# Short matmul operands filled with zero rows to 128 rows in a four-layer graph network

## The reference

```python
# layer 0: graph convolution, then a top-2 mixture of 64 experts, batch norm
m  = segment_sum((feats * rsqrt(deg_out))[src], dst) * rsqrt(deg_in)
x0 = m @ W_gc + b_gc + feats @ W_res + b_res
h1 = gelu(h @ w1[e] + b1[e]); h2 = h1 @ w2[e] + b2[e]   # for each expert e
# layer 1: mean over neighbours
x1 = feat @ w_self.T + b_self + (segment_sum(feat[src], dst) / deg) @ w_neigh.T
# layer 2: graph convolution with self loops, then a linear layer
x2 = (segment_sum((h * norm)[src], dst) + b_conv) @ W_lin + b_lin
# layer 3: tensor product on the edges, weighted by a small network of each edge's 8 scalars
w  = silu(edge_scalars @ fc_w1 / sqrt(8)) @ fc_w2 / sqrt(64)
```

## Time and profile before

| what | value |
|---|---|
| median of 3 runs | 6222.15 us (6221.89 to 6232.34) |
| span of the profiled execution | 6222.9 us |
| PE busy | 5287.1 us, 85% of the span |
| DVE busy | 3828.5 us, 62% |
| POOL busy | 3825.9 us, 61% |
| ACT busy | 1918.2 us, 31% |
| mean granted clock of TensorE | 0.850 |

### The profile page before, as it was taken

One profiled execution on the slowest core, in us unless ns is written; L12 is line 12 of the kernel. 1 busy time (PEld: TensorE's weight loads), 2 busy tenths in 40 slices (PEclk: granted clock), 3 DMA queues, 4 the chain that ended last, 5 costly groups with the idle time before them and its releaser, 6 DMA issues. The chain is left out here.

```text
span 6222.9 us, 94542 instructions
## 1 busy us (share of the span) xinstructions
PE 5287.1 (85%) x22327; PEld 3472.6 (56%) x22327; DVE 3828.5 (62%) x11568; ACT 1918.2 (31%) x5997; POOL 3825.9 (61%) x3961
## 2 busy tenths in 40 slices
PE   3689999895699994699999978998887799999998
PEld 2554444444488883444444444444333677777777
DVE  8745666556611114555555554555554799999997
ACT  0132222222022220422221242221000766666664
POOL 0157777770266651377777746777776377777771
PEclk9988888875799996888888877777565899999998
DMA  3145555552399982255555544554334366666664
GB/s 150 37 132 146 147 146 149 146 137 59 121 319 318 318 291 86 84 148 146 148 148 144 150 94 137 148 146 135 105 106 90 103 187 188 187 188 187 190 187 92
DMA packets 632253, 955.04 MB, mean 153 GB/s; under 512 B 203781, under 2 KB 472147, under 8 KB 631066
## 3 DMA queue, kind: packets, MB, share of 16 engines
q0 software_dynamic: 180864, 480.03, 28.2%
q1 hardware_dynamic: 444479, 458.06, 23.9%
q10 hardware_dynamic: 6460, 12.03, 0.6%
HBM read 772.58 MB, written 182.80 MB: 154 GB/s over the span
## 5 line engine op out<-in xcount | busy, mean ns | idle before, releaser
L688 POOL DMA_INDIRECT agg_msg<-table,agg_idx x2496 | 2362.0, 946 | 839.7 <-issue 677.5
L798 PE MATMUL bank<-agg_msg,agg_hot 128*125 128x256 f32 (+1 forms) x4992 | 1944.9, 506 | 299.5 <-DMA agg_msg<-table,agg_idx 179.4
L798 PEld LDWEIGHTS bank<-agg_msg,agg_hot 128*125 128x125 f32 x4992 | 979.5, 230 | 1246.8 <-DVE agg_hot L705 695.4
L717 DVE TENSOR_TENSOR acc<-acc,bank 125x256 f32 x2496 | 1050.3, 421 | 1005.3 <-PE bank L798 970.4
L1643 POOL DMA_INDIRECT tp_src<-table,tp_idx x832 | 920.5, 1106 | 294.8 <-issue 254.1
L1657 ACT ACTIVATE tp_hots<-tp_hot,tp_weight 128x125 f32<-128x125 f32 x2496 | 814.0, 390 | 391.3 <-PE bank L1672 362.5
L705 DVE TENSOR_SCALAR agg_hot<-iota_i,dst_w 128x126 f32<-128x126 f32 x2496 | 763.7, 306 | 0.0
L1672 PEld LDWEIGHTS bank<-tp_msg,tp_hots 128*125 128x125 f32 x4992 | 680.3, 189 | 47.7
L1672 PE MATMUL bank<-tp_msg,tp_hots 128*125 128x128 f32 x4992 | 685.0, 274 | 0.0
L826 ACT ACTIVATE agg_made<-bank,agg_made 128x128 f32<-128x128 f32 x786 | 289.0, 368 | 1256.8 <-PE bank L781 1255.2
L1668 PE MATMUL bank<-tp_msg,tp_hot 128*125 128x256 f32 x1664 | 558.5, 418 | 133.5 <-DVE tp_msg L1701 132.3
(11 more groups left out here) (286 smaller groups left out, 5519.4 us busy)
## 6 DMA issues: line engine op xcount, KB each, us to landing
tp_weight<-edge_rows SPq DMA_DIRECT2D x832, 130.0 KB, 2.3
edge_rows<-agg_made SPq DMA_DIRECT2D x262, 390.0 KB, 3.4
acc<-in_L_w_laid_dram SPq DMA_DIRECT2D x162, 512.0 KB
acc<-in_L_gnn_w_dram SPq DMA_DIRECT2D x162, 512.0 KB
agg_msg<-table,agg_idx POOLq DMA_INDIRECT x2496, 2.8
table<-tab_out SPq DMA_DIRECT2D x40, 625.0 KB
tp_src<-table,tp_idx POOLq DMA_INDIRECT x832
expert_rows<-prep_zero SPq DMA_DIRECT2D x5, 2500.0 KB
```

The costliest lines, as they stand in the source:

```text
L688: pool.indirect_dma_start(out=msg[PER * g + r][:, 0:D], out_offset=None, in_=table[:, :], in_offset=bass.IndirectOffsetOnAxis(ap=idx[g][:, ...
L717: dve.tensor_tensor(row, row, bank[0:P, 0:D], ALU.add).then_inc(s_add, 1)
L798: pe.matmul(net.bank[w % BANKS][0:P, 0:sums], hot[w % HOTS][:, 0:P], msg[w][:, :], start=True, stop=True).then_inc(s_sum, 1)
```

## The change

Operands with fewer than 128 rows get 128, with zeros in the rows that held nothing. `fc1` becomes 128 x 128, `fc2`, `scal` and `hid` get 128 partitions, so do `root_b`, `shift_b`, `b2` and the experts' `ones`. The products read all rows; L774's weights get 128 columns and its output and SiLU 128 partitions. Transfers write only the rows that they wrote before. POOL fills the aggregates' tiles with zeros at the start of each aggregate, ahead of its first gather, and SP waits for that before its first load; DVE fills the six `b2` buffers at the start of the experts, and POOL waits for these before each of the first six loads of `b2`.

```diff
-            root_w, root_b = ph.sb("root_w", [Q, 2, D]), ph.sb("root_b", [len(biases), D])
+            root_w, root_b = ph.sb("root_w", [Q, 2, D]), ph.sb("root_b", [Q, D])
...
-        fc1, fc2 = ph.sb("fc1", [8, MUL]), ph.sb("fc2", [MUL, 4, MUL])
-        scal = [ph.sb(f"scal{b}", [8, BATCH * Q]) for b in (0, 1)]
-        hid = [ph.sb(f"hid{b}", [MUL, BATCH * Q]) for b in (0, 1)]
+        fc1, fc2 = ph.sb("fc1", [Q, Q]), ph.sb("fc2", [Q, 4, MUL])
+        scal = [ph.sb(f"scal{b}", [Q, BATCH * Q]) for b in (0, 1)]
+        hid = [ph.sb(f"hid{b}", [Q, BATCH * Q]) for b in (0, 1)]
+        s_empty = ph.sem("empty")
...
             def _(pool):
+                for part in (fc1[:, :], fc2[:, :, :], scal[0][:, :], scal[1][:, :]):
+                    pool.memset(part, 0.0).then_inc(s_empty, 1)
+                if root:
+                    pool.memset(root_b[:, :], 0.0).then_inc(s_empty, 1)
+                if shift:
+                    pool.memset(shift_b[:, :], 0.0).then_inc(s_empty, 1)
...
-                    pe.matmul(side[0:P, 0:D], net.ones[0:1, 0:P], shift_b[:, :], start=False, stop=True).then_inc(s_root, 1)
+                    pe.matmul(side[0:P, 0:D], net.ones[:, 0:P], shift_b[:, :], start=False, stop=True).then_inc(s_root, 1)
...
-                    pe.matmul(zb[0:MUL, 0:BATCH * Q], fc1[:, :], scal[j % 2][:, :], start=True, stop=True).then_inc(s_z, 1)
+                    pe.matmul(zb[:, 0:BATCH * Q], fc1[:, :], scal[j % 2][:, :], start=True, stop=True).then_inc(s_z, 1)
...
-                            pe.matmul(side[0:P, 0:D], net.ones[0:len(biases), 0:P], root_b[:, :],
+                            pe.matmul(side[0:P, 0:D], net.ones[:, 0:P], root_b[:, :],
                                       start=False, stop=True).then_inc(s_root, 1)
...
             def _(sp):
+                sp.wait_ge(s_empty, 5 if root or shift else 4)
...
-            b2 = [ph.sb(f"b2_{r}", [3, D], BF16) for r in range(R)]
-            ones = ph.sb("ones", [3, Q], BF16)
+            b2 = [ph.sb(f"b2_{r}", [Q, D], BF16) for r in range(R)]
+            ones = ph.sb("ones", [Q, Q], BF16)
...
-                        pool.dma_start(b2[r][:, :], net.b2_parts[:, ds(e, 1), :].rearrange("k e d -> k (e d)")).then_inc(s_in[r], 16)
+                        if t < R:
+                            pool.wait_ge(s_empty, t + 1)
+                        pool.dma_start(b2[r][0:3, :], net.b2_parts[:, ds(e, 1), :].rearrange("k e d -> k (e d)")).then_inc(s_in[r], 16)
...
                 def _(dve):
+                    for r in range(R):
+                        dve.memset(b2[r][:, :], 0.0).then_inc(s_empty, 1)
                     dve.memset(ones[:, :], 1.0).then_inc(s_ones, 1)
```

More of the change, by code:

```diff
@@ L649, in aggregate @@
             weights, biases, to_x = root
-            root_w, root_b = ph.sb("root_w", [Q, 2, D]), ph.sb("root_b", [len(biases), D])
+            root_w, root_b = ph.sb("root_w", [Q, 2, D]), ph.sb("root_b", [Q, D])
         if shift:
             conv_b, lin_w, lin_b = shift
-            shift_c, shift_w, shift_b = ph.sb("shift_c", [Q, 1]), ph.sb("shift_w", [Q, D]), ph.sb("shift_b", [1, D])
+            shift_c, shift_w, shift_b = ph.sb("shift_c", [Q, 1]), ph.sb("shift_w", [Q, D]), ph.sb("shift_b", [Q, D])
             shift_cols = ph.sb("shift_cols", [Q, P])
@@ L816, in hidden @@
                         act.wait_ge(s_w, BATCH * (j - 1))
-                    act.activation(hid[j % 2][:, :], zb[0:MUL, 0:BATCH * Q], ACT.Silu, scale=8 ** -0.5).then_inc(s_hid, 1)
+                    act.activation(hid[j % 2][:, :], zb[:, 0:BATCH * Q], ACT.Silu, scale=8 ** -0.5).then_inc(s_hid, 1)
                 def keep(j, c):
@@ L848, in _ @@
                     sp.dma_start(shift_w[:, :], lin_w).then_inc(s_ones, 16)
-                    sp.dma_start(shift_b[:, :], lin_b.unsqueeze(0)).then_inc(s_ones, 16)
-                sp.dma_start(fc1[:, :], net.a["L3_gnn_fc_w1"][:, :]).then_inc(s_fc, 16)
+                    sp.dma_start(shift_b[0:1, :], lin_b.unsqueeze(0)).then_inc(s_ones, 16)
+                sp.dma_start(fc1[0:8, 0:MUL], net.a["L3_gnn_fc_w1"][:, :]).then_inc(s_fc, 16)
                 for k, of in enumerate(fc2_of):
-                    sp.dma_start(fc2[:, k, :], net.a["L3_gnn_fc_w2"][:, of * MUL:(of + 1) * MUL]).then_inc(s_fc, 16)
+                    sp.dma_start(fc2[0:MUL, k, :], net.a["L3_gnn_fc_w2"][:, of * MUL:(of + 1) * MUL]).then_inc(s_fc, 16)
                 def load(j):
@@ L857, in load @@
                         sp.wait_ge(s_kept[j % 2], 16 * (j // 2))
-                    sp.dma_start(scal[j % 2][:, :], net.scal_t[:, rows_of(j)]).then_inc(s_in[j % 2], 16)
+                    sp.dma_start(scal[j % 2][0:8, :], net.scal_t[:, rows_of(j)]).then_inc(s_in[j % 2], 16)
                     sp.dma_start(made[j % 2][:, :, 4 * MUL:ROW],
@@ L1363, in experts @@
             b1 = ph.sb("b1", [Q, X_EXP, KH])
-            b2 = [ph.sb(f"b2_{r}", [3, D], BF16) for r in range(R)]
-            ones = ph.sb("ones", [3, Q], BF16)
-            s_b1, s_ones = ph.sem("b1"), ph.sem("ones")
+            b2 = [ph.sb(f"b2_{r}", [Q, D], BF16) for r in range(R)]
+            ones = ph.sb("ones", [Q, Q], BF16)
+            s_b1, s_ones, s_empty = ph.sem("b1"), ph.sem("ones"), ph.sem("empty")
             rows = [ph.sb(f"rows{r}", [Q, D]) for r in range(R)]
```

## The result

The changed kernel takes 6183.45 us (median of 4 runs, 6181.04 to 6191.01); the kernel before took 6224.18 us on the same chip (6221.89 to 6232.34). The ratio is 0.9935, interval 0.9921 to 0.9949: faster by 0.65% or 40.7 us, where 49.9 were predicted; inside the predicted range (6158 to 6214) and 10 us above the predicted 6173. The profiled span is 6179.4 us, 43.5 us shorter than before.

What follows compares the result with a forecast made beforehand. Issuing gathers on POOL was taken to bound the aggregates, PE the experts. The terms -40.5 + 3.6 - 5 - 8 gave -49.9, from a span of 6222.9 to 6173 us, range 6158 to 6214.

Steps and rivals of the forecast that it cites:

- What bounds each stage: Whole kernel: issuing gathers on POOL (1.251 us each) bounds the aggregates, PE bounds the experts.
- The border of a tile: Experts, around the bias product: open weight loads cost 0.10, 0.09 and 0.06 us, in all 0.25 us a tile.
- the rival of types: Experts: the bf16 product among fp32 ones exposes the loads, not its rows; only -9.4, 6213.5 us; chance 13%.
- the rival that loads are hidden only between different rows of the array: Both stages: filling leaves every load open, nothing gained, fills remain; +3.6, 6226.5 us; chance 3%.
- the experts' term: Experts: 162 tiles shortened by 0.25 us each, -40.5 us.
- none of the other engines reaches 3.85 us a tile: Experts: transfers, POOL, ACT and DVE all need less than the new tile of 3.85 us instead of 4.10.
- the weak end: Experts: -29 us, kept in case waits between engines add 0.07 us a tile, losing 11 us.
- The 3.15 us for the transfers: Experts: transfers need 3.15 us a tile, from 1.29 MB a tile and 410 GB/s under backlog.
- The fills: Starts of three aggregates: POOL's new fills delay the first gather, 1.2 to 1.7 us each; +3.6 us, bounds 2 and 5.
- The gathers that waited for PE: First two aggregates: gathers delayed by PE at 1.2 GHz come back; -5 us, bounds 0 and -6.
- The ends: Ends of both root aggregates: fewer borders and an earlier PE, -4 each, -8 us; bounds -1.4 and -9 each.
- The clock: Aggregates, a rival: less PE work lowers the granted clock, PE becomes the bound; at 0.58 +70 us, 6243; chance 4%.

Runs made afterwards that it cites:

- e3: Changed kernel with the experts' bias product reading 64 rows instead of 128; 6219.15 us (one run).
- e4: Changed kernel with the experts' bias product reading 96 rows instead of 128; 6179.8 us (one run).
- e5: Kernel before with the experts' short bias product issued four times in a row instead of once; 6282.86 us (one run).
- e6: Changed kernel with three result buffers in the experts instead of two; 6176.42 us, ratio 0.9932 to the kernel before.
- e1: Kernel before with only the experts' part of the change (b2 and ones filled to 128 rows); 6187.64 us, ratio 0.9957.
- e2: Changed kernel without the experts' part, only the aggregates' operands filled; 6211.65 us, ratio 0.9982 to the kernel before.
- e7: Changed kernel with windows behind the last edge gathering 128 different rows instead of row 0 128 times; 6116.67 us, ratio 0.984 to the kernel before.
- e11: Changed kernel with the first product of the edge network reading 8 rows instead of 128; 6184.62 us (one run).
- e12: Changed kernel with the first product of the edge network on 64 columns of weights, all 128 rows; 6183.40 us (one run).

## Why the prediction was right

**What bounds each stage** held. POOL's gathers kept their 1.25 us, PE's busy time in the first two aggregates fell by 18% and their length by 0.3 to 0.5%; the experts shortened by what PE's sequence lost.

**The border of a tile** held in each of its three parts, 0.10, 0.09 and 0.06 us (e3, e4, e5). The changed kernel refutes the rival of types: its bf16 bias between fp32 products leaves no weight load open. It also refutes the rival that loads are hidden only between different rows of the array: both loads of the border start 0.21 and 0.11 us ahead with all products on the same 128 rows. The Trainium skill has that rule in TensorE: Matmul & The Clock Gate, The mechanism; the same section also lets a load go ahead into a background weight buffer, and with that the trace agrees.

**The size of the experts' term was off:** -36.6 in place of -40.5. The step that failed is that none of the other engines reaches 3.85 us a tile. By their busy times none does; but a scatter's round through two buffers does for some tiles, which I had left in the weak end as "waits between them" without naming it. The 3.18 us that I took for POOL's round are from issue to issue; the scatter's way to its landing, a median of 5.6 us, was not in the sum. The third buffer found it (e6). The 3.15 us for the transfers were also too easy: by the DMA share of the earlier trace rows, 0.91 of 670 us, I should have estimated 3.8 us a tile, and the changed kernel shows a share of 0.95. With three buffers the tile still takes 3.843 us, so the transfers didn't become the bound.

**The fills** cost 2.9 us (predicted 3.6). They themselves took 1.76 us in the first aggregate, a little over the 1.2 to 1.7 worked out, but only 1.4, 0.7 and 0.8 us were added in the three. The step that failed is that all of it counts: POOL had waited there before, for the first copy of indices (0.84 us in the first aggregate; in the second its first gather started 1.18 us after the stage), and part of the fills ran in that time.

```profile
2600.50 1.00 POOL L688 DMA_INDIRECT agg_msg<-table,agg_idx  x1 [64.34 <-DVE agg_idx L701]
```

**The gathers that waited for PE** came back as predicted, -6.0 against -5; the first aggregate's 1044.20 is now 1039.61, which is 831 gathers by 1.251.

**The ends** came out at -7.8 against -8, by luck more than by working. In the kernels with short products (before, e1, e5) the six ends are 24.6 to 28.7 us, on average 26.4; in five with padded ones (after, e2, e3, e4, e6) the ten are 22.7 to 25.1, on average 23.7. The change is therefore worth some 2.7 us an end, not 4 (the ends of one kind differ by up to 4 us among themselves), and the wait of 10 us that I thought an earlier PE would shorten is still 9.86. e7 shows why: the transfers there stood behind gathers of one repeated row.

**The clock** went the other way. I had argued that less work for PE means less clock and gave a rival to it. The runs show 0.95 and 0.97 where 0.84 was, with PE less busy. Of the paddings, the one from 8 rows to 128 in the first network product goes with most of the rise (e11), and the borders that it removes don't explain it (e12); what does stays open. That rival's price (a clock under 0.60) was never near.

## What to carry to other kernels

Where PE sets the pace, look for products of 64 or fewer rows, or columns of weights, among full ones: at 2.4 GHz such a product showed some 0.1 us in the open before it and 0.14 to 0.2 behind it, and zeros in the missing rows (96 were enough) took that back for a fill at the start. Short products that follow one another pay nothing for each other (e5). Where gathers set the pace the same padding gave some 10 us in three aggregates (e2, interval 4 to 19), and it is better to ask what the gathers read: padding places that all name one row cost this kernel more than all its short products.

## What the runs showed of the hardware

- Among full products at 2.4 GHz, a product of 3, 8 or 64 rows had its weight load, and that of the product behind it, in the open (steps of 0.32, 0.21 and 0.27 us around a bias product of 64 rows); one of 96 rows did not (0.22, 0.11, 0.22).
- A product on 64 columns of weights opens the weight loads too (0.53 + 0.79 us against 0.44 + 0.64), in one run.
- The granted clock in the three stretches with the edge network was 0.95 to 0.97 with all 128 rows, 0.88, 0.88 and 0.84 with 8 rows in the network's first product, and 0.97, 0.95 and 0.96 with all rows and half the columns in it, though the last two leave the same weight loads open.
- Gathers of 128 times the same row, one behind the other, land late: the last 23 of the first aggregate a median of 13.4 us after their issue, against 2.9 where as many read 128 different rows, and 23 us from the last gather to the last product against 3.
